# Second routing's first two groups inside the last state-space turns; pads, low halves and weight loads of the start reordered

## The reference

```
x = x + 0.5 * MoE(layernorm(x))          # 8 experts, top 2, hidden 512, squared relu
x = x + Mamba(layernorm(x))              # state-space block: scan over 1024 steps, 64 heads of 8, state 16
x = x + 0.5 * MoE(layernorm(x))
```

## Time and profile before

| | us |
|---|---|
| median of 3 executions | 1157.12 |
| profiled execution | 1157.05 |
| its span | 1155.0 |
| PE busy in the span | 946.3 (82%) |
| DVE busy | 914.4 (79%) |
| ACT busy | 742.8 (64%) |
| POOL busy | 589.1 (51%) |
| first expert matmul | at 85.36 |
| last state-space conv | at 818.06 to 822.08 |
| first matmul of the second experts | at 904.66 |

### The profile page before, as it was taken

One profiled execution on the slowest core, in us unless ns is written; L12 is line 12 of the kernel. 1 busy time (PEld: TensorE's weight loads), 2 busy tenths in 40 slices (PEclk: granted clock), 3 DMA queues, 4 the chain that ended last, 5 costly groups with the idle time before them and its releaser, 6 DMA issues.

```text
span 1155.0 us, 42050 instructions
## 1 busy us (share of the span) xinstructions
PE 946.3 (82%) x14928; PEld 809.8 (70%) x14928; DVE 914.4 (79%) x2840; ACT 742.8 (64%) x1751; POOL 589.1 (51%) x673
## 2 busy tenths in 40 slices
PE   2309998997988999999989899999852699989991
PEld 1209997996966777777777677777631699979990
DVE  6978885663779899999989999999878588645875
ACT  3436655563768888788888788887542376546650
POOL 4853777473644444445434444444357367745551
PEclk9999999998999999999999999999865799989995
DMA  9974565573435656666656665555424366836967
GB/s 270 285 221 89 142 160 144 123 147 84 89 89 107 125 111 116 113 121 125 124 98 118 121 125 115 112 114 96 90 65 129 76 131 144 181 91 142 217 153 236
DMA packets 199018, 154.25 MB, mean 134 GB/s; under 512 B 115808, under 2 KB 165984, under 8 KB 198688
## 3 DMA queue, kind: packets, MB, share of 16 engines
q0 software_dynamic: 43936, 72.96, 30.9%
q1 hardware_dynamic: 146816, 71.23, 26.4%
q10 hardware_dynamic: 8064, 7.38, 2.4%
HBM read 41.37 MB, written 56.10 MB: 84 GB/s over the span
## 4 chain that ended last, share of the span: by engine, by line
PE 38%; DVE 33%; issue 12%; DMA 7%; POOL 4%; ACT 3%; SPq 2%; DVEq 0%; POOLq 0%; ACTq 0%
PE bank L808 16%; PE bank L821 16%; DVE lake L1090 7%; DVE arena L1152 3%; DVE q_ L1070 2%; DVE lake L1097 2%; ACT lake L1377 2%; DMA X<-yg 2%; DMA lake<-turned_y 2%; POOL disp L656 2%; DVE lake L1131 1%; PE bank L1505 1%; PE bank L1574 1%; DVE lake L1119 1%; DMA arena<-disp 1%
## 5 line engine op out<-in xcount | busy, mean ns | idle before, releaser
L808 PE MATMUL bank<-arena,weights 128*128 128x128 f16 x3744 | 242.2, 223 | 63.6 <-DMA arena<-disp 60.6
L808 PEld LDWEIGHTS bank<-arena,weights 128*128 x3744 | 227.7, 100 | 68.9 <-issue 66.0
L755 POOL DMA_INDIRECT ychosen<-arena,didx x156 | 160.6, 1029 | 182.3 <-issue 99.1
L821 PE MATMUL bank<-weights,arena 128*128 x1872 | 232.6, 275 | 2.4 <-DVE arena L929 2.4
L862 ACT ACTIVATE arena<-bank 128x512 f32<-128x512 f32 x156 | 93.2, 598 | 206.1 <-PE bank L808 183.5
L924 DVE TENSOR_TENSOR arena<-arena 128x512 f32<-128x512 f32 x156 | 107.8, 691 | 139.1 <-ACT arena L862 132.0
L821 PEld LDWEIGHTS bank<-weights,arena 128*128 128x128 f16 x1872 | 178.4, 99 | 22.0 <-issue 2.7
L656 POOL DMA_INDIRECT disp<-lake,sloti x128 | 133.2, 1041 | 42.2 <-issue 37.2
L1090 DVE SCALAR_TENSOR_TENSOR lake<-lake,vec 128x128 f32<-128x128 f32 x480 | 128.8, 343 | 0.0
L1239 POOL DMA_DIRECT2D lake<-turned_y x32 | 27.3, 855 | 189.8 <-DMA turned_y<-lake 175.5
L929 DVE TENSOR_TENSOR arena<-arena 128x512 f16<-128x512 f32 x156 | 108.0, 692 | 5.3
(11 more groups left out here) (177 smaller groups left out, 1934.1 us busy)
## 6 DMA issues: line engine op xcount, KB each, us to landing
arena<-in_w SPq DMA_DIRECT2D x16, 512.0 KB, 10.1
yg<-ychosen SPq DMA_DIRECT2D x32, 256.0 KB, 2.8
X<-yg POOLq DMA_DIRECT2D x64, 128.0 KB, 3.6
arena<-lake SPq DMA_DIRECT2D x128, 64.0 KB, 3.3
lake<-lake POOLq DMA_DIRECT2D x32, 256.0 KB, 4.2
turned_y<-lake SPq DMA_DIRECT2D x128, 64.0 KB, 1.8
lake<-turned_y POOLq DMA_DIRECT2D x32, 256.0 KB, 4.2
lake<-ychosen SPq DMA_DIRECT2D x32, 256.0 KB, 3.8
```

The source lines that it names most:

```text
L755: pool.indirect_dma_start(ychosen, bass.IndirectOffsetOnAxis(ap=didx[:, t % NIDX:t % NIDX + 1], axis=0), ysb[n % YB][:, :], None).then_inc ...
L808: mm = pe.matmul(o, chunk(where, 2 * ("hl".index(w) * WN + c * HID + m * P), P), v, start=c == 0 and n_ == 0, stop=c == KD - 1 and n_ == 2)
L821: mm = pe.matmul(down_ps(n), x, chunk(where, 2 * ((2 + "hl".index(w)) * WN + c * D), D), start=c == 0 and n_ == 0, stop=c == KH - 1 and n_ ...
```

## The change

1. Start, DVE: `place_rows(0)` stands before `low(1)`; the statistics of groups 6 and 7 stand after the last 16 low halves.
2. Start, ACT: the odd pads stand before the last 16 high halves (label "halved").
3. SP: the weights and vectors of the state-space block are issued one by one behind tile loads 26 to 34 of the first experts.
4. Second routing: group 0 gets buffers of its own (rows in the arena, normalised values in yg, ranks in a free part of bank 2), groups 0 and 1 share `first_xT` and bank 0 for the transposes, and are worked half by half on PE.
5. DVE: stats of groups 0 and 1 after the last conv in turn 30, norm(0) and low(0) at the end of turn 30; stats(2), choose(0), norm(1) before `gate_in(31)`, then place(0), low(1), stats(3), choose(1), place(1) at the end of turn 31.
6. ACT: rows(0) at the end of turn 30; evictions of group 0 before `out_of_heads(31)`; the rest of group 0 and the evictions of group 1 at the end of turn 31. PE: transposes and logits of group 0 before `intra(31)`; ranks(0), transposes and logits of group 1 and ranks(1) at the end of turn 31.
7. POOL: the powers of groups 0 and 1 in turn 30; the 8 scatters of group 0 before `add_turned(31)`.

The diff, cut to its core:

```diff
         xo = [carve(D), sb("xo", [P, D])]
+        first_rows32 = carve(GT_ * ROW // 2)
+        first_rows = first_rows32.bitcast(F16)
+        first_xT = carve(2 * 2 * D, F16)
...
+        def early(r, g):
+            return r == 1 and g < 2
+        def xh_of(r, g, h):
+            return yg[h][:, :] if r == 1 and g == 0 else xh[pair(g, h) % 4]
+        def turned_ps(r, g, h):
+            return banks[0 if early(r, g) else h][:, :]
...   # route_dve
-            if r:
-                dve.wait_ge(S("m_intra"), NT)
             norm(0)
+            yield ("norm", 0)
             low(0)
+            yield ("low", 0)
             for g in range(NG):
...
-                if g + 1 < NG:
+                if g + 1 < NG and not early(r, g):
                     norm(g + 1)
                 choose(g)
+                if g == 0 and r:
+                    norm(g + 1)
+                    yield ("norm", g + 1)
+                if g == 0 or early(r, g):
+                    place_rows(g)
+                    yield ("placed", g)
+                if g == 1 and r:
+                    norm(g + 1)
                 if g + 1 < NG:
                     low(g + 1)
-                place_rows(g)
+                if g and not early(r, g):
+                    place_rows(g)
...
                 if g == HG - 1:
-                    for late in range(HG + 2, NG):
-                        stats(late)
                     if r == 0:
                         for k in range(2 * NCHUNK, 4 * NCHUNK):
                             split_low(dve, k)
+                    for late in range(HG + 2, NG):
+                        stats(late)
...   # route_act, rows(g)
+                if r and g == 1:
+                    act.wait_ge(S("m_intra"), NT)
...   # route_pe
+            def half_by_half(g):
+                for h in range(2):
+                    turned_rows(g, [h])
+                    logits(g, [h])
+            if r:
+                pe.wait_ge(S("m_ee"), NT)
+                pe.wait_ge(S("m_bt"), NT)
+                pe.wait_ge(S("m_cb"), NT)
+                yield from half_by_half(0)
...
+                if g == 1 and r:
+                    pe.wait_ge(S("m_gz"), NT)
                 ranks(g)
-                if g == 0 and r:
+                if g == 1 and r:
                     pe.wait_ge(S("m_GT"), NT)
                     pe.wait_ge(S("m_x"), NT)
...   # SP
-        SP_TURNS = {50: ("load", 0), 51: ("load", 1), 58: ("load", 2), 62: ("load", 3)}
+        SP_TURNS = {26: ("weights", "wo"), 28: ("weights", "wz"), 30: ("weights", "wx"), 32: ("weights", "wbc"), 33: ("weights", "wdt"),
+                    34: ("weights", None), 50: ("load", 0), 51: ("load", 1), 58: ("load", 2), 62: ("load", 3)}
...   # mamba_dve
+                if i == NT - 2:
+                    until(routing, ("stats", 1))
                 if i == NT - 1:
-                    until(routing, ("stats", 1))
+                    until(routing, ("norm", 1))
                 if inside(i):
                     gate_in(i)
...
+                if i == NT - 2:
+                    until(routing, ("low", 0))
                 if i == NT - 1:
-                    until(routing, ("place", 0))
+                    until(routing, ("placed", 1))
...   # mamba_pool
+                if i == NT - 2:
+                    until(routing, ("power", 1))
                 if i == NT - 1:
-                    until(routing, ("power", 1))
+                    until(routing, ("sent", 0, 2 * GT_ - 1))
                 if inside(i):
                     add_turned(i)
-                if i == NT:
-                    until(routing, ("sent", 0, 2 * GT_ - 1))
                 if inside(i - 1):
                     add_out(i - 1)
...   # mamba_act
+                if i == NT - 1:
+                    until(routing, ("turned", 0))
                 if inside(i):
                     out_of_heads(i)
...   # mamba_pe
+                if i == NT - 1:
+                    until(routing, ("logits half", 0, 1))
                 if inside(i):
                     intra(i)
...
                 if i == NT - 1:
-                    until(routing, ("ranks", 0))
+                    until(routing, ("ranks", 1))
```

More of the change, by code:

```diff
@@ L393, in place_rows @@
             def place_rows(g):
-                p, ranks = g % 2, rank_ps
+                p, ranks = g % 2, ranks_of(r, g)
                 dve.wait_ge(S("rank_ps"), g0 + g + 1)
@@ L530, in route_act @@
             rows(0)
+            yield ("rows", 0)
             turned_rows(0)
+            yield ("turned", 0)
             for g in range(NG):
+                if g == 0 and r:
+                    ratio(g)
+                    yield ("ratio", g)
                 if g + 1 < NG:
@@ L555, in route_pe, with turned_rows @@
                 pe.wait_ge(S("rw_low"), 1)
-            def turned_rows(g):
-                for h in range(2):
+            def turned_rows(g, halves=range(2)):
+                for h in halves:
                     q = 2 * g0 + pair(g, h)
                     pe.wait_ge(S("lo"), q + 1)
-                    if q >= 2:
+                    if early(r, g):
+                        pe.wait_ge(S("xt"), q)
+                    elif q >= 2:
                         pe.wait_ge(S("xt"), q - 1)
-                    to = banks[h][:, :].bitcast(F16)
+                    to = turned_ps(r, g, h).bitcast(F16)
                     for x in range(2):
@@ L567, in turned_rows, with logits @@
                             m = pe.transpose(to[:, (x * 2 * KD + c) * P:(x * 2 * KD + c + 1) * P],
-                                             drow[g % HG][:, at:at + P], ident16)
+                                             rows_of(r, g)[:, at:at + P], ident16)
                     m.then_inc(S("xt_ps"), 1)
-            def logits(g):
-                for h in range(2):
+            def logits(g, halves=range(2)):
+                for h in halves:
                     q = 2 * g0 + pair(g, h)
@@ L576, in logits @@
                         pe.wait_ge(S("ohb"), g0 + g)
+                    if r and g == 1:
+                        pe.wait_ge(S("slot"), g0 + g)
                     for x in range(2):
@@ L853, in experts_act @@
             pads(act, 2 * r, range(1, E, 2))
+            if r == 0:
+                until(routing, ("halved",))
             def relu(s):
@@ L1296, in move @@
                                  y1[j * QT:(j + 1) * QT, :].rearrange("t (b c) -> t b c", b=B)).then_inc(S("m_yw"), 16)
+            yield from mamba_load(sp)
             sp.wait_ge(S("stage_used"), 4 * NCHUNK)
+            yield ("weights", None)
             sp.dma_start(upto[:, :], a["upto"]).then_inc(S("m_upto"), 16)
@@ L1492, in mamba_act @@
                     turned_b(i + 1)
+                if i == NT - 2:
+                    until(routing, ("rows", 0))
                 if i == NT - 1:
-                    until(routing, ("ratio", 0))
+                    until(routing, ("turned", 1))
         def mamba_pe(pe, routing):
```

59 lines of the change are left out of this document (39 added, 20 removed).

## The result

The changed kernel took 1166.68 us, the median of 7 executions (1163.65 to 1167.62); the kernel before, run beside it, took 1157.12 (7 executions, 1155.01 to 1161.12). The ratio is 1.0066, 95% interval 1.0050 to 1.0082, so some 7.6 us slower. The profiled execution took 1165.58 with a span of 1163.6, 8.6 us more than before's 1155.0. The prediction was 1162.0 with 1154 to 1168: the direction is right, the size 2.7 to 4.7 us short.

A forecast was written before the change was run, and what follows sets the result against it. The second routing was taken as bound by POOL, the start by DVE's wait for the first tile. Start -6.2 and turns +11.1 gave +4.9 us on 1157.05, so 1162.0, with an 8-in-10 range of 1154 to 1168.

The forecast's parts named there:

- The turns: Second routing, turns 30 and 31: group 1's scatters on POOL begin at 877.4 instead of 866.27, loss 11.1 us.
- the early groups pay: Rival, second routing: group 0's scatters, if begun before 842.1, fill POOL's idle time in turn 31; 1147 us, chance 0.12.
- The start: First routing to first expert work: earlier pads and tile load bring DVE's work from 88.83 to 82.6, gain 6.2 us.
- four of them took 4.14 us there, so all eight are issued by 67.6: Start, pads on SP and ACT: both begin at about 63.5, with ACT's earlier 4.14 us for four as the price.
- The DVE shift: Start, DVE: placing group 0 before low(1) makes the following work 1.75 us later, bounds 0.7 and 1.9.
- my low bound of 4.1: Start: the gain in us if the landings are slow, against 6.2 forecast.
- From there on DVE, then PE, carry it through: After DVE's first expert work: the start's gain of 6.2 us lasts through the rest of the kernel.
- the slower one: Rival: scatters land at 77, start gains 4.1; PE at half clock, turns lose 13.5; 1166.5 us, chance 0.25.
- The parts cancel: Rival, whole kernel: start gives 7.2, DVE's added work hides in turn 30, turns lose 7.4; 1157 us, chance 0.23.
- The two rules: Skill rules: 256 KB GpSimd DMA takes 2.6 us, sum 1.5 lower; TensorE slows after pauses, sum at upper bound.

The follow-up runs named there:

- logits_early: Changed kernel with gate(31) before choose(1), add_out(31) behind both groups' scatters, group 0's logits before project_out(30): 1154.44 us, ratio 0.9963 to the kernel before.
- sp_pads: Changed kernel with all eight pads of the first part on SP and none on ACT: one execution, DVE's first expert work at 83.07 against 85.73.
- start_only: Kernel before with only the start's part of the change (parts 1 to 3), turns as before: median 1156.59 us, ratio 0.9996.

## Why the prediction was right, and where it was off

**The turns, forecast +11.1, measured +9.7: the mechanism as described, one term too long.** Counted from the last conv, forecast and measured: group 0's first scatter 35.1 and 33.2; from there to add_turned(31) 10.2 and 10.2; its landing 4.4 and 4.3; over gate, projection and finish to add_out(31) 7.0 and 7.1; to group 1's first scatter 2.4 to 2.6 and 2.6; sum 59.3 and 57.5. Only the first is off, by 1.9 us, and it splits: project_out(30) came 3.1 us later behind the conv than before, not 3.75 (19.5 became 22.6), so a little more of DVE's added work hid in its own waits than I let it; and the two halves on PE and ACT took 3.9 us where I put 5.2. One half took 1.94 us on PE (its transposes from 838.03, the next half's from 839.97), where I had counted some 2.6: the transposes were 0.61 and not 0.9, and the hand-overs shorter. Behind group 1's first scatter 38.8 us follow instead of 38.4, which I put at nothing.

**What that means for "the early groups pay".** I gave it 0.12 and asked for scatters before 842.1, which is 24.0 behind the conv. They came 33.2 behind it. logits_early shows that my condition was too strict: with scatters at 850.4 (31.9 behind the conv) the whole is faster than before, because there add_turned(31) is ahead of them and add_out(31) behind both groups. The condition holds for the order that the change has, not for the idea.

**The start, forecast -6.2, measured -3.1 at DVE and -0.5 +- 1.8 at the end.** The step that failed is "four of them took 4.14 us there, so all eight are issued by 67.6". SP's four held it for 4.34 us, ACT's for 7.74. I had priced ACT's pads as issues, and for pads alone their end decides little, since the last landing was in range (first load 76.1, forecast 73.6 with 77.5 as the bound); but the high halves stand behind them on ACT, and DVE's low halves behind those. sp_pads shows it: 83.07 with the pads gone from ACT, where the forecast was 82.6. The DVE shift itself was right: 0.68 us for the ranks, the wait for the high halves with row 26.21 for 24.50 (1.7 us, forecast 1.75), last scatter 69.76 (forecast 70.0). The pads are the shared cause of load and list: my low bound of 4.1 held only the load's side of it. A second step failed too: "From there on DVE, then PE, carry it through". start_only has the 3.1 us at DVE and is not measurably faster at the end.

**The sum.** +4.9 was forecast, +7.6 +- 1.8 measured. The turns gave 1.4 less and the start 3.1 to 5.7 less than forecast, by its place or by the total. Of the rivals, the slower one (1166.5: start 4.1, turns 13.5) comes nearest in time, but not by its mechanism for the turns, as PE ran the projection at half clock in both kernels (3.78 us in the earlier trace rows and above). It was right in saying that the start gives little. The total lies in the range although the start's term came out below its own lower bound of 4.1, since the turns cost less than forecast: that part is luck, and that the change is slower rests on the turns. "The parts cancel" fails by the turns' 9.7.

**The two rules.** add_turned's 256 KB landed 4.2 us after its issue in the median of the changed kernel and 4.3 on its critical piece, against an estimate of 2.6 by the Trainium skill, DMA: Bandwidth & Descriptors, Anatomy of one DMA; the trace of before was the better guide. The added pauses of the turns hardly lowered TensorE's clock further: in the 35 us from the start of the last conv its mean is 0.81 against 0.74 before, and from 850 to 900 us 0.50 against 0.53 in the earlier trace rows. At one place they did, with little effect: silu(31)'s four transposes behind an idle time of 5.80 us took 1.12 us, against 0.66 behind 2.23 before. The row at 93 us shows a fall behind a pause of 1.6 us in three profiles and none in four others with the same pause; the Trainium skill, TensorE: Matmul & The Clock Gate, A second HAM failure mode, has short idling between groups of matmuls make the clock swing, which fits the three and doesn't tell them from the four.

## What to carry to other kernels

Work brought forward on an in-order engine is only early if what the old work is waiting for doesn't stand behind it: list for every engine what is queued behind the moved block and who waits for that, and put short instructions that start a long landing (here add_turned) ahead of it and those that end a chain (add_out) behind. A DMA issue on a computing engine's queue is not a fixed small cost: four issues held ACT for 7.74 us, one of them for 4.43, so they belong on an engine that has nothing else to do. And a gain at the start of a program is to be followed to the end before it is counted.

## What the hardware showed

- The same zero-row DMA holds its issuing queue for very different times: four took 4.14 us on ACT before, 7.74 in the changed kernel (the first alone 4.43) and 9.13 with the weights' traffic beside them. Eight on SP alone took at most 0.40 each, with the DMA engines as busy as in the changed kernel (0.99). The Trainium skill, DMA: Bandwidth & Descriptors, Anatomy of one DMA, calls descriptor generation small for POOL's kind of DMA. What the 4.43 us on ACT's queue are made of, no run here shows.
- A scatter's price does not follow the DMA load: most take 0.97 us and 0.30 us to the next, 1.27 together, at 69.76 us with the DMA engines full (share 1.02 from 65 to 70) as at 858.06 (0.32 from 855 to 860). A few take up to 1.3.
- One chip ran the kernel before once, in 1229.49 us and at a mean granted clock of 0.950, where it took a median of 1157 to 1158 at 0.950 to 0.957 otherwise, so versions are to be set beside the kernel before on the same chip.
